# Where q and k are normalised: three scaled ScalarE copies, or one VectorE multiplication by a broadcast reciprocal root

## What is computed

```python
q = _fp8_linear_pertensor(ln_out, wq, wq_scale, q_in_scale).reshape(b, s, g, hpg, d)
q = _ln(q, qln_w, qln_b)                      # over d = 128, per token and head
k = _fp8_linear_pertensor(ln_out, wk, wk_scale, k_in_scale).reshape(b, s, g, d)
k = _ln(k, kln_w, kln_b)
v = _fp8_linear_pertensor(ln_out, wv, wv_scale, v_in_scale).reshape(b, s, g, d)
core = _gqa(q, k, v).reshape(b, s, nh * d)    # softmax(q k^T / sqrt(d)) v
qx = _ln(_fp8_linear_pertensor(ln_out, wqx, ...), qxln_w, qxln_b)
kx, vx = jnp.split(jnp.einsum('bsi,oi->bso', cond, w_kv_x), 2, axis=-1)   # kx through _ln too
xout = _gqa(qx, kx, vx).reshape(b, s, nh * d)
```

## Time and profile before

| | |
|---|---|
| median of 3 runs | 1968.98 us (1964.92 to 1971.75) |
| span of the profiled execution | 1968.4 us |
| PE busy | 1697.1 us, 86% |
| DVE busy | 1440.0 us, 73% |
| ACT busy | 1402.7 us, 71% |
| POOL busy | 1151.5 us, 58% |
| mean granted TensorE clock | 0.978 of full |

### The profile page before, as it was taken

One profiled execution on the slowest core, in us unless ns is written; L12 is line 12 of the kernel. 1 busy time (PEld: TensorE's weight loads), 2 busy tenths in 40 slices (PEclk: granted clock), 3 DMA queues, 4 the chain that ended last, 5 costly groups with the idle time before them and its releaser, 6 DMA issues.

```text
span 1968.4 us, 48001 instructions
## 1 busy us (share of the span) xinstructions
PE 1697.1 (86%) x15776; PEld 1239.6 (63%) x15776; DVE 1440.0 (73%) x3227; ACT 1402.7 (71%) x2926; POOL 1151.5 (58%) x1045
## 2 busy tenths in 40 slices
PE   0015899999999999999999999999999579999998
PEld 0004677877777777778777777777877344444443
DVE  7996698799789879978987997898777533323232
ACT  3335889998988989899898989889999634021211
POOL 3454677777777777777777777777777403020201
PEclk9998999999999999999999999999999889999999
DMA  4100486887787778778777876877888982022000
GB/s 145 53 32 1 90 151 122 142 156 136 124 145 143 130 131 155 137 122 147 145 127 132 154 136 121 146 143 130 151 170 156 277 238 103 29 100 103 25 21 21
DMA packets 639377, 240.83 MB, mean 122 GB/s; under 512 B 612496, under 2 KB 612496, under 8 KB 638608
## 3 DMA queue, kind: packets, MB, share of 16 engines
q1 hardware_dynamic: 639120, 237.62, 59.8%
HBM read 65.57 MB, written 20.97 MB: 44 GB/s over the span
## 4 chain that ended last, share of the span: by engine, by line
issue 42%; POOL 29%; PE 5%; ACT 4%; DMA 2%; POOLq 1%; SPq 0%; DVE 0%; ACTq 0%
POOL local L975 14%; POOL head_rstd L951 7%; POOL local L958 5%; POOL local L989 3%; PE ps_pj L562 2%; DMA local<-local 2%; ACT local L841 1%; ACT local L838 1%; ACT local L764 1%; PE ps_s L695 1%; PE ps_s L696 1%; PE ps_s L626 0%; PE ps_o L612 0%; PE ps_s L627 0%; PE ps_s L628 0%
## 5 line engine op out<-in xcount | busy, mean ns | idle before, releaser
L975 POOL TENSOR_TENSOR local<-local 128x512 bf16<-128x512 f32 x512 | 605.9, 1183 | 372.4 <-ACT local L841 372.2
L562 PE MATMUL ps_pj<-wide 128*128 (+2 forms) x5544 | 587.8, 255 | 9.6 <-ACT local L764 7.9
L562 PEld LDWEIGHTS ps_pj<-wide 128*128 128x128 bf16 x5544 | 471.6, 99 | 124.9 <-issue 8.2
L612 PE MATMUL ps_o<-v_hi,local 128*128 128x129 bf16 x2048 | 381.8, 224 | 59.5 <-DMA local<-local 39.0
L838 ACT ACTIVATE local<-ps_s,neg_max 128x512 f32<-128x512 f32 x512 | 382.1, 746 | 63.6 <-DVE neg_max L1187 60.6
L841 ACT ACTIVATE local<-ps_s,neg_max 128x512 bf16<-128x512 f32 x512 | 384.2, 750 | 14.1 <-DMA local<-local 14.1
L1187 DVE TENSOR_REDUCE neg_max<-ps_s 128x1 f32<-128x512 f32 x512 | 345.9, 676 | 64.9 <-PE ps_s L628 64.5
L614 PE MATMUL ps_o<-v_hi,local 128*128 128x129 bf16 x2048 | 381.2, 221 | 0.0
L613 PE MATMUL ps_o<-local 128*128 128x128 bf16 x2048 | 380.9, 220 | 0.0
L764 ACT ACTIVATE local<-ps_pj,head_rstd 128x128 f32<-128x128 f32 x756 | 235.2, 423 | 40.3 <-issue 38.2
L612 PEld LDWEIGHTS ps_o<-v_hi,local 128*128 128x128 bf16 x2048 | 200.8, 98 | 79.0 <-DVE local L1195 31.1
(11 more groups left out here) (111 smaller groups left out, 2745.1 us busy)
## 6 DMA issues: line engine op xcount, KB each, us to landing
w_raw<-w_group SPq DMA_DIRECT2D x32, 512.0 KB, 4.1
quantised_heads<-local SPq DMA_DIRECT2D x32, 512.0 KB, 3.4
wide<-quantised_heads SPq DMA_DIRECT2D x4, 4096.0 KB, 13.8
local<-local SPq DMA_TRANSPOSE x640, 3.2
local<-x SPq DMA_DIRECT2D x4, 1024.0 KB, 5.2
local<-ctx_t SPq DMA_DIRECT2D x4, 1024.0 KB, 5.0
w_raw<-w_proj SPq DMA_DIRECT2D x8, 512.0 KB, 4.7
wide<-w_proj SPq DMA_DIRECT2D x4, 1024.0 KB, 6.0
```

Of the source, the lines that this page charges most:

```text
L562: last = mm(dst[:, at:at + n], lhs, w_at(par, part, c, cross * 512 + at, n), start=(k == 0), stop=(k == len(terms) - 1))
L612: mm(acc, ph, vh, start=(tc == 0), stop=False)
L975: tt_(pp[:, u % PP_BUFS, 1], p_exp[:, u % 2], pp[:, u % PP_BUFS, 0], ALU.subtract)\
```

## The change

The multiplication of a tile goes from ACT to DVE. `head_norm` is now one `tensor_tensor` over 384 columns: the PSUM bank times `head_rstd`, three numbers per partition, each repeated over its 128 columns by a broadcast access pattern. It waits for the root and for the transposes; that the rest of v is done no longer needs a semaphore, since the same engine does both. Semaphore counts and the engines that wait for them stay as they were.

```diff
@@ ScalarE
-            def head_norm(i, t, turns):
-                act.wait_ge(vlo_done, t + 1)
-                act.wait_ge(rstd_done, t + 1)
-                if not isinstance(t, int) or t >= TILES:
-                    act.wait_ge(qt_done, turns)
-                for h in range(3):
-                    hs = slice(h * D, (h + 1) * D)
-                    last = a(qn[:, i, hs], tile_bank(i, t)[:, hs], ACT.Copy, scale=head_rstd[:, i % 2, h:h + 1])
-                last.then_inc(qn_done, 1)
...
-                    head_norm(i - 1, i - 1, 0)
...
-            head_norm(TILES - 1, TILES - 1, 0)
...
-                    for k in tile_at(slot, QN_LAG, first, last):
-                        head_norm(tile_place(k)[1], GROUP_TILES * g + TILES + k, GROUP_TURNS * g + 3 * (1 + k // TT))
@@ VectorE
+            def head_norm(i, t, turns):
+                dve.wait_ge(rstd_done, t + 1)
+                if not isinstance(t, int) or t >= TILES:
+                    dve.wait_ge(qt_done, turns)
+                v.tensor_tensor(qn[:, i].rearrange("p (h d) -> p h d", h=3),
+                                tile_bank(i, t)[:, 0:3 * D].rearrange("p (h d) -> p h d", h=3),
+                                head_rstd[:, i % 2, 0:3].unsqueeze(2).to_broadcast([P, 3, D]), ALU.mult).then_inc(qn_done, 1)
...
+                head_norm(i, i, 0)            # start, behind v_rest and the quantising of the last chunks
...
+                    for k in tile_at(slot, QN_LAG, first, last):     # pipeline, right behind L1195 of the slot
+                        head_norm(tile_place(k)[1], GROUP_TILES * g + TILES + k, GROUP_TURNS * g + 3 * (1 + k // TT))
```

## The result

The changed kernel takes 2134.59 us (median of 4 runs, 2133.56 to 2135.65), the kernel before 1969.58 us beside it: 1.085 times as long, 95% interval 1.0829 to 1.087. Forecast were 2124 us.

The account below looks back on a forecast made before the run. PE sets the pace now; DVE's wait for POOL's root closes a ring. Groups 1 to 6 +118, group 0 +22, group 7 +14, start +1: 155 us on 1968.4, forecast 2124 us, 8 in 10 within 2045 to 2170.

Parts of the forecast that it names:

- The root comes too late for DVE: POOL's root is ready 1.67 and 1.66 us behind the end of L1195, where DVE's new multiplication stands.
- The multiplication's size: DVE's new instruction of 384 columns takes 0.55 us and holds DVE for 0.50 us, 16 us a group.
- The ring: DVE's multiplication, row maximum, ACT's exponentials, POOL's L975 and root, next multiplication: 4.69 us a tile, 6.49 with quantising.
- The sum for a group: Ring 178.9 us plus L1051, L1226, loop's end and queues: 191.4 against 171.7, +19.7, for six groups +118 us.
- the loop's end: DVE's standing at the loop's end adds between 0 and 3.7 us a group to the ring; 2.2 taken.
- The two small terms for DVE's and ACT's queues: ACT's work ahead of exponentials and DVE's ahead of sums of squares (slots 16, 36): 0 to 6 us a group, 1.5 taken.
- the start: First eight tiles, with reduce, root and multiplication one after another on DVE: 0 to 4 us, 1 taken.
- Before, the same instructions were no ring.: In the kernel before, the ring's instructions closed no ring, because DVE never waited for the root.
- ACT's relief at nothing: Removing 768 copies, 238.8 us, from ACT gains nothing, since another engine sets the pace.
- Only DVE's work: Rival, chance 0.07: root in time, only DVE's work where weights are prepared costs, 20 us in all; 1989 us.
- The rule of the Trainium skill: Saturation decides, so the change costs next to nothing outside the weight preparation; the first rival, 1989 us, chance 0.07.
- Faster: Rival, chance 0.06: ACT held PE back, and PE gets some 34 of 57 us idle time back; 1935 us.

Follow-up runs that it names:

- the root first in both kernels: POOL's root put ahead of the slot's L975: in the changed kernel 1955.18 us (0.9937), in the kernel before 1946.17 us (0.9895).
- half of it, well placed: Changed kernel with POOL's root ahead of L975, multiplications of even tiles on DVE, of odd tiles as copies on ACT: 1926.75 us, 0.9806 of the kernel before.
- the first three experiments: Changed kernel without the wait for this tile's root, 1965.05 us; kernel before with only that wait added, 2112.54; changed kernel with POOL's root ahead of L975, 1955.18.

## Why the prediction was right, point by point

*The root comes too late for DVE.* Right: 1.62, 0.94 and 1.54 us of idle ahead of three multiplications, where 1.67 and 1.66 us of lateness were read before. The idle time is what the round leaves over when DVE's own instructions are taken off: 0.94 stands in the round in which DVE also has an L1204, which holds it for 0.60 us (936.61 to 937.21), and 1.54 in one without.

*The multiplication's size.* Right: 556 ns where 0.55 us was taken from the line between 128 and 512 columns.

*The ring.* Right, and shown: its links stand in the trace, one added instruction lengthens it by its own time, and it opens when POOL's order is changed. 4.60 and 6.39 us for 4.69 and 6.49; DVE starts 0.04 us behind POOL's end (939.78 to 939.82), not the 0.08 that ACT took.

*The sum for a group.* 191.4 forecast, 193.7 measured, and partly by luck, since two errors offset each other. The ring alone is 16 x (11.18 - 10.99) = 3.0 us a group shorter than summed, and the pieces beside it are 17.8 us in place of 12.5. How the 17.8 divides can be read from the starts of all multiplications of groups 1 to 6, each period less 4.60 or 6.39. The four L1036 add 7.0 us where 5.5 were taken, since L1051's 1.38 us had become 1.76 (the last section). The reciprocal L1223 adds 3.3, as forecast, and the loop's end 2.4 for 2.2. The two small terms for DVE's and ACT's queues, taken at 1.5 together, came to 4.4: 1.7 in slots 20 and 40, where four L1027 stand on DVE ahead of the sum of squares (slots 16 and 36, which the prediction named, added nothing); 1.0 in slots 24 and 44, where ACT has a weight copy; and 1.7 in slots 28 and 48, where ACT's squares waited 1.13 and 1.40 us for PE's projection in group 4, a link that the prediction does not have. 0.7 is spread over the rest. Groups 1 to 6 gave 132 us for 118, group 0 20 for 22, group 7 11 for 14, the start 0.2 for 1.

*"Before, the same instructions were no ring."* Wrong. It was one through ACT, 4.71 us, not hidden at 55 of 256 tiles, and opening it was worth 20 us. The forecast did not hang on it, but a reader of that sentence would have missed the better change.

*ACT's relief at nothing.* No run takes the copies off ACT and leaves all else, so this term has no measurement of its own. With the root first in both kernels the relief is worth less than the multiplication costs on DVE, by 0.4% (0.9937 against 0.9895).

*The rivals.* "Only DVE's work" named 1989 us as the price of the work; measured with the wait gone it is 1965, though against a kernel with 20 us of its own to gain. The rule of the Trainium skill (Perfetto Trace Analysis, section Optimizing Scalar/DVE Operations) that was set against the trace speaks of saturated engines. DVE was not saturated in groups 1 to 6 of the changed kernel (82% busy, and PE at least 87%), and it lost 8.5%. With the wait gone the runs agree with the rule as far as they go: leaving the copies on ACT was 0.4% better than DVE's multiplication, and doing that one twice cost 37 us, with DVE busy 1013.99 of 1050.2 us in groups 1 to 6. "Faster" named 1935 us if DVE's wait were under 0.4 us a tile; with that wait at nothing the whole move came to 1955, and half of it, well placed, to 1927.

## What to carry to other kernels

When a step is moved to another engine, its wait moves too: follow what stands behind the waiting instruction round to what it waits for, and if that comes back, add up the links; their sum is the pace, whatever the busy shares say. A wait alone, without work, was enough for 7.3% here. And look at the order on the engine that is waited for, before the work is moved: two instructions swapped there were worth 20 us with nothing moved at all.

## What the runs showed of the hardware

DVE's L1051 (float32 and bf16, both from SBUF, 1024 columns) is the same instruction in both kernels, L1036 in the changed one:

```profile
L1036 DVE TENSOR_TENSOR wide<-w_raw,wide 128x1024 f32 x24 | 42.3, 1764 | 0.0
```

1764 ns in place of 1378. It meets an instruction of POOL's in both kernels; what differs is which of the two starts first. In group 4, DVE's row and then POOL's:

```profile
1016.01 1.63 DVE L1036 TENSOR_TENSOR wide<-w_raw,wide 128x1024 f32 x1
```

```profile
1015.47 1.09 POOL L943 TENSOR_TENSOR local<-local 128x512 bf16<-128x512 f32 x1
1016.52 2.14 POOL L960 TENSOR_TENSOR local<-local 128x512 bf16<-128x512 f32 x1
```

L943 was there first and keeps its 1.09 us, to 1016.56; L1036 ends 1.08 us behind it. L960, which takes 1.16 us otherwise, starts while L1036 runs, and ends 1.02 us behind that one's end. The one that starts second is longer, the first is not. So it is in all 140 cases of this instruction in both kernels and the first three experiments: where POOL's had started before, DVE's ended 1.07 to 1.09 us behind it, and where L960 (or its equal) started second, it ended 1.00 to 1.03 us behind DVE's. Where both start within 0.04 us, either can be the longer one. Before, DVE was first in 23 of 28 cases (1.21 or 1.22 us); in the changed kernel POOL was first in 27 (1.63 or 2.17 us). The Trainium skill (SBUF — State Buffer, section Who interferes with whom) says that a VectorE instruction with two SBUF inputs contends with a GpSimd one that reads SBUF; these rows agree. It also says that one with a single SBUF input does not: the new multiplication, PSUM and SBUF, took 540 to 559 ns in all 256 cases, 233 of them beside an L943 or L960, which agrees too. No run changes this overlap and nothing else. In the kernel with the multiplication twice DVE's instruction starts half a microsecond later, when POOL's is ending, and takes 1.22 us in 21 of 28 cases.
